# Attention scores on the two row halves of the TensorE array: three products of 64 rows each in place of two of 128 rows, in a two-layer attention kernel

## What is computed

```python
xn = group_norm(xf, norm_w, norm_b)
qkv = jnp.einsum('oc,bct->bot', qkv_w, xn) + qkv_b[None, :, None]
q, k, v = (qkv[:, :ch], qkv[:, ch:2 * ch], qkv[:, 2 * ch:])       # per head, ch = 64
weight = jnp.einsum('bct,bcs->bts', q * scale, k * scale)          # 1024 x 1024 per head
weight = jax.nn.softmax(weight.astype(jnp.float32), axis=-1)
a = jnp.einsum('bts,bcs->bct', weight, v).reshape(b, c, T)
hout = jnp.einsum('oc,bct->bot', proj_w, a) + proj_b[None, :, None]
return (xf + hout).reshape(b, c, H, W)
```

## Time and profile before

| | |
|---|---|
| median of three executions | 4349.01 us (4347.39 to 4350.95) |
| span of the profiled execution, first to last instruction | 4346.0 us |
| outside the span (median less span) | 3.0 us |
| busy: PE / VectorE / ScalarE / GpSimd | 4295.6 / 3313.6 / 2875.3 / 2505.1 us |
| mean granted TensorE clock | 0.999 |

### The profile page before, as it was taken

The page is one execution under the profiler, slowest core; times in us unless marked ns, Lnnn a source line. Parts: engine busy times, 40 slices in busy tenths (PEclk is TensorE's granted clock), DMA queues, the critical chain, the costliest instruction groups (busy, mean ns, idle before and its releaser), DMA issues.

```text
span 4346.0 us, 89905 instructions
## 1 busy us (share of the span) xinstructions
PE 4295.6 (99%) x26692; PEld 3736.9 (86%) x26692; DVE 3313.6 (76%) x5483; ACT 2875.3 (66%) x5317; POOL 2505.1 (58%) x2406
## 2 busy tenths in 40 slices
PE   7999999999999999999999999999999999999999
PEld 6888888888888888888888888888888888888887
DVE  5777867788687786777867778687786877868778
ACT  4757747477474775747757476574765747667476
POOL 5655556565564655656566565565655646556465
PEclk9999999999999999999999999999999999999999
DMA  3232222322223222222222222222222222223222
GB/s 87 48 96 47 71 72 48 96 47 80 64 46 96 49 78 64 56 86 49 80 71 66 81 46 80 65 66 79 48 79 64 71 71 49 79 64 82 60 49 92
DMA packets 99933, 295.61 MB, mean 68 GB/s; under 512 B 15136, under 2 KB 15264, under 8 KB 99616
## 3 DMA queue, kind: packets, MB, share of 16 engines
q1 hardware_dynamic: 99616, 291.71, 25.0%
HBM read 123.88 MB, written 33.55 MB: 36 GB/s over the span
## 4 chain that ended last, share of the span: by engine, by line
PE 95%; DVE 2%; issue 1%; POOL 1%; ACT 1%; DMA 0%; SPq 0%; DVEq 0%; ACTq 0%; POOLq 0%
PE ps_t L760 21%; PE ps_g L714 15%; PE ps_o L772 11%; PE ps_o L773 11%; PE ps_s L751 11%; PE ps_s L749 11%; PE ps_s L714 7%; PE ps_t L714 6%; PE ps_o L714 3%; POOL x_raw L389 1%; ACT probs L479 0%; DVE spread L603 0%; DVE pt_lo L569 0%; DVE work L601 0%; PE ps_t L778 0%
## 5 line engine op out<-in xcount | busy, mean ns | idle before, releaser
L383 POOL TENSOR_SCALAR probs<-probs,row_rcp 128x1024 f32<-128x1024 f32 x1024 | 1149.9, 1123 | 1375.5 <-DVE row_rcp L564 1374.0
L560 DVE TENSOR_REDUCE row_min<-ps_s 128x1 f32<-128x1024 f32 x1024 | 1250.2, 1221 | 220.5 <-PE ps_s L751 205.0
L484 ACT CAST pt_hi<-ps_t 128x512 fp32r<-128x512 f32 x2048 | 1110.6, 590 | 446.5 <-PE ps_t L760 431.7
L569 DVE TENSOR_TENSOR pt_lo<-ps_t,pt_hi 128x512 fp32r<-128x512 f32 x2048 | 1308.5, 679 | 9.5 <-ACT pt_hi L484 5.0
L479 ACT ACTIVATE probs<-ps_s,row_min 128x1024 f32<-128x1024 f32 x1024 | 1150.7, 1124 | 215.5 <-DVE row_min L560 202.5
L760 PEld LDWEIGHTS ps_t<-const_sb,probs 128*128 128x128 f32 x8192 | 944.3, 140 | 185.5 <-DVE pt_lo L569 57.0
L760 PE MATMUL ps_t<-const_sb,probs 128*128 128x128 f32 x8192 | 1085.9, 274 | 0.8
L772 PE MATMUL ps_o<-pt_hi,v_st 128*128 128x256 f32 x4096 | 1044.4, 288 | 0.0
L773 PE MATMUL ps_o<-pt_lo,v_st 128*128 128x256 f32 x4096 | 1014.8, 282 | 0.0
L751 PE MATMUL ps_s<-kl_st,q_st 128*128 128x512 f32 x2048 | 808.3, 395 | 0.0
L772 PEld LDWEIGHTS ps_o<-pt_hi,v_st 128*128 128x128 f32 x4096 | 771.6, 188 | 39.4 <-issue 12.4
(11 more groups left out here) (110 smaller groups left out, 4918.2 us busy)
## 6 DMA issues: line engine op xcount, KB each, us to landing
wqk_raw<-in_wqk SPq DMA_DIRECT2D x130, 256.0 KB, 2.7
q_st<-kh_st SPq DMA_DIRECT2D x128, 256.0 KB, 2.9
q_st<-kl_st SPq DMA_DIRECT2D x128, 256.0 KB, 3.6
kh_st<-kh_st SPq DMA_DIRECT2D x128, 256.0 KB, 2.9
kl_st<-kl_st SPq DMA_DIRECT2D x128, 256.0 KB, 3.5
x_raw<-layer_out SPq DMA_DIRECT2D x36, 512.0 KB, 5.0
wv_raw<-in_wv SPq DMA_DIRECT2D x68, 256.0 KB, 3.6
x_raw<-in_x SPq DMA_DIRECT2D x32, 512.0 KB, 5.3
```

What stands on the lines that cost most here:

```text
L383: nc.gpsimd.tensor_scalar(probs[m % 2][:, :], probs[m % 2][:, :], row_rcp[:, m % 4:m % 4 + 1], 1.0, ALU.mult, ALU.mult).then_inc(probs_rea ...
L484: nc.scalar.copy(pt_hi[:, m // 2 % 2, 4 * half:4 * half + 4, (m % 2) * P:(m % 2 + 1) * P], ps_t[:, half, :].rearrange("p (b t) -> p b t", ...
L560: nc.vector.tensor_reduce(row_min[:, m % 4:m % 4 + 1], ps_s[:, m % 2, :], AX.X, ALU.min).then_inc(min_ready, 1)
L569: nc.vector.tensor_tensor(pt_lo[place], ps_t[:, half, :].rearrange("p (b t) -> p b t", b=4), f32(pt_hi[place]), ALU.subtract).then_inc(lo_ ...
```

## The change

The stacking goes. `hi_st` and `lo_st` are what `split_qk` writes: q in rows 0 to 63 and k in rows 64 to 127, high and low. `hi_sw` and `lo_sw` are the same with the halves swapped: q in rows 64 to 127, and the first 512 keys of k in rows 0 to 63. The matmuls for the first half of the keys then contract over rows 0 to 63 and those for the second half over rows 64 to 127, each into its own bank of PSUM. Each half takes three products (hi*hi, lo*hi, hi*lo), so that a tile is six matmuls of 64 rows and 512 columns, alternating between the two row halves. `stack` issues four DMAs without a wait between them, two of 256 KB and two of half that size. V's bias isn't added when V leaves PSUM (`evac_v` becomes a copy) but in `add_halves`, as a scalar per partition; the broadcast `bv_all` goes, and a small `bv_sb` is loaded in its place.

```diff
-                sp.dma_start(f32(q_st[s][0:D, :]), f32(kh_st[s][0:D, :])).then_inc(q_moved, 16)
-                sp.dma_start(f32(q_st[s][D:P, :]), f32(kl_st[s][0:D, :])).then_inc(q_moved, 16)
-                sp.wait_ge(q_moved, 32 * (hd + 1))
-                sp.dma_start(f32(kh_st[s][0:D, :]), f32(kh_st[s][D:P, :])).then_inc(stacked[s], 16)
-                sp.dma_start(f32(kl_st[s][0:D, :]), f32(kl_st[s][D:P, :])).then_inc(stacked[s], 16)
+                for swapped, straight in ((hi_sw, hi_st), (lo_sw, lo_st)):
+                    sp.dma_start(f32(swapped[s][D:P, :]), f32(straight[s][0:D, :])).then_inc(stacked[s], 16)
+                    sp.dma_start(f32(swapped[s][0:D, 0:HALF]), f32(straight[s][D:P, 0:HALF])).then_inc(stacked[s], 16)
...
-            sp.dma_start(bv_all[:, :, :], bv.rearrange("(o l) n -> o l n", o=1).broadcast_to([P, LAYERS, C])).then_inc(const_loaded, 16)
+            sp.dma_start(bv_sb[:, :], bv).then_inc(const_loaded, 16)
...
-                nc.vector.tensor_tensor(attn[rows, cols], ps_o[rows, 0:GROUP], o_part[k % 2][rows, :],
-                                        ALU.add).then_inc(attn_ready, 1)
+                nc.vector.scalar_tensor_tensor(out=attn[rows, cols], in0=ps_o[rows, 0:GROUP],
+                                               scalar=bv_sb[rows, bass.ds(lay * KT + p, 1)], in1=o_part[k % 2][rows, :],
+                                               op0=ALU.add, op1=ALU.add).then_inc(attn_ready, 1)
...
-                nc.vector.tensor_tensor(v_raw[:, b, :].rearrange("p (o n) -> p o n", o=1),
-                                        v_bank[b].rearrange("p (o n) -> p o n", o=1),
-                                        bv_all[:, bass.ds(lay, 1), :], ALU.add).then_inc(v_evac, 1)
+                nc.vector.tensor_copy(v_raw[:, b, :], v_bank[b]).then_inc(v_evac, 1)
...
-                for half in range(2):
-                    cols = slice(half * HALF, (half + 1) * HALF)
-                    nc.tensor.matmul(ps_s[:, m % 2, cols], q_st[s][:, j * P:(j + 1) * P], kh_st[s][:, cols],
-                                     start=True, stop=False)
-                    mm = nc.tensor.matmul(ps_s[:, m % 2, cols], q_st[s][:, j * P:(j + 1) * P], kl_st[s][:, cols],
-                                          start=False, stop=True)
+                tile = slice((m % NT) * P, (m % NT + 1) * P)
+                top, low = slice(0, D), slice(D, P)
+                first, second = slice(0, HALF), slice(HALF, T)
+                for n, (q, k) in enumerate(((0, 0), (1, 0), (0, 1))):
+                    nc.tensor.matmul(ps_s[:, m % 2, first], (hi_st, lo_st)[q][s][top, tile],
+                                     (hi_sw, lo_sw)[k][s][top, first], start=n == 0, stop=n == 2)
+                    mm = nc.tensor.matmul(ps_s[:, m % 2, second], (hi_sw, lo_sw)[q][s][low, tile],
+                                          (hi_st, lo_st)[k][s][low, second], start=n == 0, stop=n == 2)
                 mm.then_inc(scores_ready, 1)
```

More of the change, by code:

```diff
@@ L102, in build @@
         qk = sb("qk", [P, T], F32)
-        q_st = [sb(f"q_st{s}", [P, T], F32R) for s in range(2)]
-        kh_st = [sb(f"kh_st{s}", [P, T], F32R) for s in range(2)]
-        kl_st = [sb(f"kl_st{s}", [P, T], F32R) for s in range(2)]
+        hi_st = [sb(f"hi_st{s}", [P, T], F32R) for s in range(2)]
+        lo_st = [sb(f"lo_st{s}", [P, T], F32R) for s in range(2)]
+        hi_sw = [sb(f"hi_sw{s}", [P, T], F32R) for s in range(2)]
+        lo_sw = [sb(f"lo_sw{s}", [P, T], F32R) for s in range(2)]
         v_raw = sb("v_raw", [P, BLK, C], F32)
@@ L113, in build @@
         stage = probs + [sb(f"stage{s}", [P, T], F32) for s in range(2)]
-        bv_all = sb("bv_all", [P, LAYERS, C], F32)
         const_sb = sb("const_sb", [P, 2 * P], F32)
@@ L119, in build @@
         bo_sb = sb("bo_sb", [P, LAYERS * KT], F32)
+        bv_sb = sb("bv_sb", [P, LAYERS * KT], F32)
         nw_sb = sb("nw_sb", [P, LAYERS * KT], F32)
         nb_sb = sb("nb_sb", [P, LAYERS * KT], F32)
[L122 to L125, removed]
+        row_stats = sb("row_stats", [P, 16], F32)
+        qk_scale = row_stats[:, 12:13]
+        row_min, row_sum, row_rcp = (row_stats[:, 4 * n:4 * n + 4] for n in range(3))
         bn_part = sb("bn_part", [P, KT, 12], F32)
@@ L163, in build @@
         wv_loaded = [sem(f"wv_loaded{s}") for s in range(2)]
-        q_moved = sem("q_moved")
         stacked = [sem(f"stacked{s}") for s in range(2)]
@@ L369, in split_qk @@
                 wait_alone(pool, qk_evac, 2 * hd + half + 1)
-                nc.gpsimd.tensor_scalar(kh_st[s][:, cols], qk[:, cols], 1.0, 1.0, ALU.mult, ALU.mult).then_inc(qk_hi_done, 1)
+                nc.gpsimd.tensor_scalar(hi_st[s][:, cols], qk[:, cols], 1.0, 1.0, ALU.mult, ALU.mult).then_inc(qk_hi_done, 1)
                 pool.wait_ge(qk_hi_done, 2 * hd + half + 1)
-                nc.gpsimd.tensor_tensor(kl_st[s][:, cols], qk[:, cols], f32(kh_st[s][:, cols]),
+                nc.gpsimd.tensor_tensor(lo_st[s][:, cols], qk[:, cols], f32(hi_st[s][:, cols]),
                                         ALU.subtract).then_inc(qk_split, 1)
@@ L570, in low_part, with add_halves @@
                                         f32(pt_hi[place]), ALU.subtract).then_inc(lo_ready, 1)
-            def add_halves(pair, k):
+            def add_halves(pair, lay, p, k):
                 rows = slice(0, D) if k < 4 else slice(D, P)
@@ L627, in x_low, with evac_v @@
                                         ALU.subtract).then_inc(xn_ready, 1)
-            def evac_v(i, lay, b):
+            def evac_v(i, b):
                 dve.wait_ge(v_acc, 8 * i + b + 1)
-                nc.vector.tensor_tensor(v_raw[:, b, :].rearrange("p (o n) -> p o n", o=1),
-                                        v_bank[b].rearrange("p (o n) -> p o n", o=1),
-                                        bv_all[:, bass.ds(lay, 1), :], ALU.add).then_inc(v_evac, 1)
+                nc.vector.tensor_copy(v_raw[:, b, :], v_bank[b]).then_inc(v_evac, 1)
             def output(i, lay, q):
@@ L662, in _, with pair_steps @@
                 x_low(0, c)
-            def pair_steps(i, p, last):
+            def pair_steps(i, lay, p, last):
                 pair = PAIRS * i + p
@@ L668, in pair_steps @@
                     if not last and m >= 4 and m % 2 == 0:
-                        add_halves(pair, m // 2 - 2)
+                        add_halves(pair, lay, p, m // 2 - 2)
                     if not (last and m + 2 >= PT_STEPS):
@@ L674, in pair_steps @@
                     if m == PT_STEPS - 1 or last and m >= 3 and m % 2 == 1:
-                        add_halves(pair, (m - 3) // 2)
+                        add_halves(pair, lay, p, (m - 3) // 2)
                     if not (last and m + 2 >= PT_STEPS):
@@ L685, in pair_steps @@
                     group_spread(i + 1)
-                add_halves(pair, 7)
+                add_halves(pair, lay, p, 7)
             with dve.Fori(0, PASSES) as i:
@@ L690, in _ @@
                 for b in range(4):
-                    evac_v(i, lay, b)
+                    evac_v(i, b)
                 for m in range(2):
                     smallest(TILES * i + m, m)
-                    evac_v(i, lay, 4 + 2 * m)
+                    evac_v(i, 4 + 2 * m)
                     reciprocal(TILES * i + m, m)
-                    evac_v(i, lay, 5 + 2 * m)
+                    evac_v(i, 5 + 2 * m)
                 with dve.Fori(0, PAIRS - 1) as p:
-                    pair_steps(i, p, False)
-                pair_steps(i, PAIRS - 1, True)
+                    pair_steps(i, lay, p, False)
+                pair_steps(i, lay, PAIRS - 1, True)
                 norm_coefs(i + 1, within(next_pass(i) // B, 0, LAYERS - 1))
@@ L744, in scores @@
             def scores(m, s):
-                j = m % NT
-                for half in range(2):
-                    cols = slice(half * HALF, (half + 1) * HALF)
-                    nc.tensor.matmul(ps_s[:, m % 2, cols], q_st[s][:, j * P:(j + 1) * P], kh_st[s][:, cols],
-                                     start=True, stop=False)
-                    mm = nc.tensor.matmul(ps_s[:, m % 2, cols], q_st[s][:, j * P:(j + 1) * P], kl_st[s][:, cols],
-                                          start=False, stop=True)
+                tile = slice((m % NT) * P, (m % NT + 1) * P)
[6 more added lines that the diff above has]
+                                          (hi_st, lo_st)[k][s][low, second], start=n == 0, stop=n == 2)
                 mm.then_inc(scores_ready, 1)
@@ L813, in pair_steps @@
                             if j == NT - 2:
-                                pe.wait_ge(stacked[s], 32 * (4 * i + p + 1 + e))
+                                pe.wait_ge(stacked[s], 64 * (4 * i + p + 1 + e))
                             scores(m + 2, s)
@@ L858, in _ @@
                     qk_part(half, qk_bank[1][half], 1, 0, 3 * KT)
-                pe.wait_ge(stacked[0], 32 * (4 * i + 1))
+                pe.wait_ge(stacked[0], 64 * (4 * i + 1))
```

(2 more changed lines are left out.)

## The result

The changed kernel takes 4451.04 us (median of 4, 4449.1 to 4451.82) beside 4348.27 for the kernel before (a median of 4 too, 4347.39 to 4350.95): 1.0235 times as long, 95% interval 1.022 to 1.0249. It is slower by 103 us, where 4267 us had been forecast.

A forecast was written before the change was run, and what follows sets the result against it. TensorE was taken as the bound; 4346.0 - 88 (scores) - 1 (start) + 7 (V's bias) = 4264 us of span, plus 3.0 for the median, 4267 us. Its own range was 4215 to 4335, the range with rivals 4170 to 4500.

The forecast's parts named there:

- The bound: Whole kernel: TensorE is the bound, busy 4295.6 of 4346.0 us, scores 0.93 us a tile; in pair 3 VectorE is.
- Side by side: Score matmuls: if the two row halves work side by side, six matmuls are three pairs of 0.23 us, 0.23 less a tile.
- The rival of serial halves: Score matmuls: the halves run one after the other, 0.47 us more a tile, 4767 us; chance 0.07.
- The offset of 0.11 us: Within a score pair: one weight load runs ahead, so the second matmul starts 0.11 us later and the block ends 0.11 later.
- rival (a): Score pairs: both halves truly together, no offset, 0.23 us a tile less, 4186 us or 4171; chance 0.24.
- The change of shape at 0: Both ends of a score block: switching the array between 128 and 64 rows costs 0, range up to 0.27 us a change.
- the signs of being wrong: Prediction wrong if a change of shape costs over 0.06 us, or VectorE's waits for scores vanish in pairs 0 to 2.
- Rival (b): Ends of score blocks: shape changes empty the engine, 0.16 us each with loads hidden; 4499 us, without offset 4390; chance 0.28.
- How many tiles: Score savings: 46 tiles in each of 16 passes give 0.12 us, 88 us less; pair 3 gives only some two tiles.
- V's bias: `evac_v` and `add_halves` on VectorE: 0.05 us more a sum, hidden in pairs 0 to 2; 7 us on the path.
- The moves: DMAs of the swapped halves: four stay four with less to carry, nothing gained or lost, 0.
- The start: TensorE's first matmul: waits for `bv_all` until 12.10 us; with 4 KB in its place 1.1 us go.

The follow-up runs named there:

- four_products: The changed kernel with lo*lo as a fourth product of each half, so four pairs of 64-row matmuls a tile: 4678.22 us, 1.0763.
- rows64_unpaired: The kernel before, its two score matmuls with kl_st cut to rows 0 to 63 and put after the two with kh_st: 4667.66 us, 1.0735.

## Why the prediction was wrong, step by step

**The bound** was right: TensorE, with the scores as 0.93 us a tile, and VectorE near it in pair 3 only. The loss in pair 3 is 0.5 us for 14 tiles, as its waits took up 1.2 of 1.7.

**Side by side** was right: three pairs at 0.23 us, which save 0.23 us a tile; four_products measured the pair again. The rival of serial halves fell.

**The offset of 0.11 us** was wrong, and too careful: it is 0.00. I had read from the earlier trace rows that one load runs ahead, but all the loads there go to the same rows. Here two loads for different row halves run side by side (both at 1027.75), a thing that a trace of 128-row matmuls can't show. This was rival (a), for which the Trainium skill spoke (TensorE: Matmul & The Clock Gate, Part 3, The mechanism); the trace agrees, with starts within 0.01 us.

**The change of shape at 0** is the step that failed, and it alone turned the sign. I took the change from transposes to plain matmuls for a change of kind, but both use 128 rows, so that row said nothing of the case. It measures 0.20 us on the way in and 0.15 on the way out in the changed kernel, and 0.34 for both in rows64_unpaired. That lies between my ends of 0 and 0.54 for the two, and nearer the upper. Of the signs of being wrong the first came true, a change of over 0.06 us; the second didn't, as VectorE's wait for scores stayed (205.0 us before, 204.0 after).

Rival (b) was right, in the form without the offset. That its 0.32 us for two changes came so near is in part luck: its delay of 0.16 a change is 0.09 to 0.10, and its loads, taken as hidden, are bare by 0.11 in and 0.05 out. A tile costs 0.12 us more, not 0.09. By that rival's own sum this would be 4420 us, where I had written 4390 and 4499 for two forms; the rest up to 4451 is that all 64 tiles of a pass pay, not 62, and that the waits in pair 3, which it took to hide 3 us a pass, hid 1.2. The rule of the Trainium skill (TensorEngine Tiling (Array Packing), Key Properties) that a switch of mode drains the TensorE names no price. The runs agree that each switch costs time, 0.09 to 0.10 us of delay and a load that doesn't go ahead; whether the array is empty in between, no row shows. I gave this rival 0.28, and the forecast, which needed both a free change and a full offset, 0.36; the rule was the only evidence on a real change of shape, and I let a row on another matter outweigh it.

**How many tiles**: 46 of 64 was the count for a gain. For a loss nearly all of pairs 0 to 2 count: 5.39 us a pass are 0.11 for each of 48 tiles. The rest of the 6.41 comes from pair 3 and the start of a pass. That the third tile and pair 3 absorb was right.

**V's bias**: the 7 us on the path came out as 13 alone and as 3 at most beside the slower scores. The mechanism was right (0.062 us a sum, 0.05 forecast); the place was wrong, since most of the 13 us lie in pairs 0 to 2, which I had taken for covered.

**The moves** cost nothing, as said: no wait of TensorE for them stands in the list. **The start**: TensorE's first matmul comes 0.8 us earlier in place of 1.1, as the statistics then came last, at 11.14 us (10.94 before):
```profile
10.70 0.44 DVE L569 BATCH_NORM_AGGREGATE bn<-bn_part 128x2 f32<-128x12 f32 x2
11.26 0.50 PEld L757 LDWEIGHTS ps_t<-bn,const_sb 128*128 128x128 f32 x2 [11.26 <-DMA bv_sb<-in_bv]
11.29 0.56 PE L757 MATMUL ps_t<-bn,const_sb 128*128 128x4 f32 x2 [11.29 <-DVE bn L569]
```
The gain doesn't last: the first transposes of the run come at 64.06 us, where they came at 63.59.

## What to carry to other kernels

Two matmuls on the two row halves do run in the time of one, but each block of them between 128-row matmuls costs a fixed 0.34 to 0.35 us, about 0.17 for each change of shape: here a block must save more than one and a half steps of 512 columns before it pays. When the trace holds no instance of a resource's change, a row of another kind of change is not the nearest bound; price it by both ends and let the sign stay open. And an operation that is free beside one bound isn't free beside another: measure the parts of a change both together and apart.

## What the runs showed of the hardware

- Matmuls of 64 rows and 512 columns on different row halves start within 0.01 us of each other, with their weight loads side by side. Inside a block a pair follows the one before at 0.23 us; only the second follows the first at 0.34.
- They do so even when the program lists three of one half before three of the other (4458 against 4451 us).
- A change between 128 and 64 rows delays the next matmul by 0.09 to 0.10 us, and its weight load doesn't go ahead, 0.05 to 0.11 us more. It needs no pairs: two lone 64-row matmuls a tile cost 0.34 us (3.79 against 3.45).
- On VectorE a copy of 128x512 out of PSUM takes as long as a sum with a second operand (692 and 691 ns); the sum with a scalar per partition took 483 ns where the plain one took 421, on 64x256.
